# Moving the carry of the last 64 tokens' keys and values from ScalarE to SyncE's DMA queue

## The reference

```
xn = layernorm(x)
out = x + attn_block(xn) + ffn_block(xn)
```

```
q, k, v = split(shift_token(x) @ wqkv)          # 512 columns each
q, k = rotary_xpos(l2norm(q) * qs, l2norm(k) * ksc)
# windows of 64 tokens; each window's queries see the keys and
# values of their own window and of the window before
attn = softmax(mask(q k^T)); o = attn @ v
x = x + o @ wo
x = x + gated_ffn(layernorm(shift_token(x)))
```

## Time and profile before

| | |
|---|---|
| three runs, us | 990.7, 990.86, 988.4 (median 990.7) |
| the profiled execution, us | 988.95 |
| its span in the profile, us | 986.8 |
| busy: PE, DVE, ACT, POOL, us | 868.8, 685.1, 691.4, 623.8 |
| mean granted clock of TensorE | 0.98 |

### The profile page before, as it was taken

One profiled execution on the slowest core, in us unless ns is written; L12 is line 12 of the kernel. 1 busy time (PEld: TensorE's weight loads), 2 busy tenths in 40 slices (PEclk: granted clock), 3 DMA queues, 4 the chain that ended last, 5 costly groups with the idle time before them and its releaser, 6 DMA issues.

```text
span 986.8 us, 26415 instructions
## 1 busy us (share of the span) xinstructions
PE 868.8 (88%) x10836; PEld 582.5 (59%) x10836; DVE 685.1 (69%) x1129; ACT 691.4 (70%) x1419; POOL 623.8 (63%) x492
## 2 busy tenths in 40 slices
PE   1678889989899998998989889999999999999876
PEld 0346666666656666566666656565656565656552
DVE  5874665757667576675666877888787878797733
ACT  0456786877868777687786667777777777777643
POOL 4488676776767767767576566657575757575500
PEclk9979999999999999999999899999999999999987
DMA  9100000000000000000000000000000000000000
GB/s 291 28 1 3 2 2 2 2 3 2 3 2 1 3 1 3 2 2 3 1 3 2 1 1 2 2 12 12 13 12 7 17 2 22 1 23 2 22 23 11
DMA packets 20481, 13.47 MB, mean 14 GB/s; under 512 B 4578, under 2 KB 19596, under 8 KB 20236
## 3 DMA queue, kind: packets, MB, share of 16 engines
q1 hardware_dynamic: 15108, 10.49, 3.5%
q10 hardware_dynamic: 5256, 1.31, 0.8%
HBM read 9.70 MB, written 2.10 MB: 12 GB/s over the span
## 4 chain that ended last, share of the span: by engine, by line
PE 51%; DVE 23%; ACT 14%; issue 8%; POOL 3%; DMA 1%; DVEq 0%; POOLq 0%; SPq 0%; ACTq 0%
PE pQK L1172 6%; DVE m L711 6%; PE pS L1098 5%; PE pT L1083 4%; PE pT L1040 4%; PE pM L1115 4%; PE pV L1135 4%; PE pM L1245 4%; PE pS L1072 4%; PE pQK L1336 3%; DVE xa L899 2%; DVE ss L724 2%; DVE pr L759 2%; DVE mx L757 2%; PE pS L1059 2%
## 5 line engine op out<-in xcount | busy, mean ns | idle before, releaser
L355 POOL TENSOR_TENSOR rn<-rn,half_neg 128x16 f32<-128x16 f32 x64 | 187.5, 2929 | 5.3
L368 POOL TENSOR_TENSOR m<-m 128x1024 f32<-128x1024 f32 x64 | 151.0, 2359 | 1.0 <-DVE m L711 1.0
L353 POOL TENSOR_SCALAR rn<-ss 128x16 f32<-128x16 f32 x64 | 16.3, 255 | 205.1 <-DVE ss L724 203.9
L375 POOL TENSOR_TENSOR qkn<-m,rn 128x1024 f32<-128x1024 f32 x64 | 123.7, 1933 | 5.0
L757 DVE TENSOR_REDUCE mx<-pS 128x8 f32<-128x1024 f32 x64 | 78.1, 1220 | 66.7 <-PE pS L1072 66.6
L1172 PE MATMUL pQK<-wqkv,hT 128*128 128x512 f32 x256 | 123.5, 606 | 0.8 <-DVE m L711 0.8
L510 ACT ACTIVATE kT<-pT 128x512 f32<-128x512 f32 x64 | 38.1, 595 | 86.4 <-PE pT L1040 85.9
L550 ACT ACTIVATE sq<-pQK 128x1024 f32<-128x1024 f32 x64 | 65.4, 1021 | 25.7 <-PE pQK L1172 25.6
L724 DVE TENSOR_REDUCE ss<-sq 128x16 f32<-128x1024 f32 x64 | 77.5, 1210 | 5.4 <-ACT sq L550 5.3
L1098 PE MATMUL pS<-vmix,prT 128*64 128x65 f32 x1024 | 74.0, 226 | 7.4 <-DVE pr L759 7.4
L1098 PEld LDWEIGHTS pS<-vmix,prT 128*64 128x64 f32 x1024 | 65.3, 139 | 25.5 <-issue 20.8
(11 more groups left out here) (169 smaller groups left out, 2038.2 us busy)
## 6 DMA issues: line engine op xcount, KB each, us to landing
x<-in_L_attn_x SPq DMA_DIRECT2D x4, 512.0 KB, 9.4
xs<-in_L_attn_x SPq DMA_DIRECT2D x8, 256.0 KB, 2.8
out<-aqkT SPq DMA_DIRECT2D x8, 256.0 KB, 2.2
wqkv<-in_L_ffn_wqkv SPq DMA_DIRECT2D x2, 768.0 KB, 9.5
tab<-in_k_tab SPq DMA_DIRECT2D x1, 1024.0 KB, 10.5
w<-in_L_ffn_w SPq DMA_DIRECT2D x2, 341.0 KB, 10.3
wo<-in_L_ffn_wo SPq DMA_DIRECT2D x2, 256.0 KB
cst<-in_k_cst ACTq DMA_DIRECT2D x1, 404.5 KB, 4.0
```

The lines of the kernel that those rows point to most:

```text
L355: eng.tensor_tensor(rn[:, k % 2, :], rn[:, k % 2, :], half_neg[:, 0:2 * H], ALU.pow).then_inc(S["rn_done"], 1)
L368: eng.tensor_tensor(m1[:, k % 2, :], m1[:, k % 2, :], m2[:, :], ALU.add).then_inc(S["add_done"], 1)
L375: eng.tensor_tensor(qkn[:, k % 2, :].rearrange("p (h d) -> p h d", d=DH), m1[:, k % 2, :].rearrange("p (h d) -> p h d", d=DH), rn[:, k % 2 ...
```

## The change

The two copies leave ScalarE's stream. SP issues them as DMAs from SBUF to SBUF, one pair per tile from the second tile on, each behind a wait for the semaphore that ScalarE had waited for: o_mm for the values, s_mm for the keys. A completed DMA adds 16 to its semaphore, so ScalarE's two waits count in sixteens. The value DMA copies whole rows of 520 fp32 per partition (65 for each head, with the constant ones that form the softmax sum), where ScalarE copied 8 runs of 64. The key DMA copies 4 runs of 64 fp32 in each of 128 partitions. SP's loop over the output steps is written out over the bodies: `xs` is loaded at the start of the body, the body's four carries follow, and then the wait for `osb` and the store.

```diff
--- before.py
+++ after.py
@@ -298,6 +298,13 @@
             body(None, None, (1, NT - 1))
 
 
+        def sp_carry(sp, n, b):
+
+            sp.wait_ge(LS["o_mm"], n - 3)
+            sp.dma_start(vmix[b][64:P, :, :], vown[b][64:P, :, :]).then_inc(LS["v_kept"], 16)
+            sp.wait_ge(LS["s_mm"], n - 3)
+            sp.dma_start(kT[b][:, :, P:P + WIN], kT[b][:, :, WIN:P]).then_inc(LS["carried"], 16)
+
         @block.sync
         def _(sp):
             for b in range(NB):
@@ -312,16 +319,20 @@
                 sp.dma_start(w2[:, l, 0:2, :], a["L0_ffn_w2"][l, 0:2 * P, :].rearrange("(c p) d -> p c d", p=P)).then_inc(w_ld, 16)
                 sp.dma_start(w2[0:CHUNKS[2][1], l, 2, :], a["L0_ffn_w2"][l, 2 * P:HID, :]).then_inc(w_ld, 16)
 
-            sp.dma_start(xs[:, :, :], x_steps[0]).then_inc(G["xs"], 16)
-            sp.wait_ge(G["osb"], 1)
-            sp.dma_start(out_steps[0], osb[:, :, :]).then_inc(G["out"], 16)
-            with sp.Fori(1, NT) as t:
-                sp.wait_ge(G["out"], 16 * t)
-                sp.dma_start(xs[:, :, :], x_steps[t]).then_inc(G["xs"], 16)
-                sp.wait_ge(G["osb"], t + 1)
-                sp.dma_start(out_steps[t], osb[:, :, :]).then_inc(G["out"], 16)
+            def body(new, old, ff):
+                last = ff and ff[0] == 1
+                if last:
+                    need(sp, G["out"], 16 * ff[1])
+                    sp.dma_start(xs[:, :, :], x_steps[ff[1]]).then_inc(G["xs"], 16)
+                for k in range(NB):
+                    if new and not is_start(new):
+                        sp_carry(sp, count(new, k), k)
+                if last:
+                    sp.wait_ge(G["osb"], ff[1] + 1)
+                    sp.dma_start(out_steps[ff[1]], osb[:, :, :]).then_inc(G["out"], 16)
+
+            run_bodies(sp, body)
             sp.wait_ge(G["out"], 16 * NT)
-
 
         def pool_slot(eng, new, old, k):
 
@@ -506,22 +517,17 @@
                 step, b, m = turned
                 eng.wait_ge(S["t_mm"], 2 * m + 1)
                 if not is_start(step):
-                    eng.wait_ge(S["carried"], m - 3)
+                    eng.wait_ge(S["carried"], 16 * (m - 3))
                 eng.activation(kT[b][:, :, 0:P], pT[:, 512:1024].rearrange("p (c n) -> p c n", c=4), ACT.Copy).then_inc(S["t_ev"], 1)
                 eng.wait_ge(S["t_mm"], 2 * m + 2)
                 eng.activation(qT[:, :, :], pT[:, 0:512].rearrange("p (c n) -> p c n", c=4), ACT.Copy).then_inc(S["t_ev"], 1)
             if new:
-                if not is_start(new):
-
-                    need(eng, S["o_mm"], n - 3)
-                    eng.activation(vmix[k][64:P, :, 0:DH], vown[k][64:P, :, 0:DH], ACT.Copy).then_inc(S["v_kept"], 1)
-                    eng.activation(kT[k][:, :, P:P + WIN], kT[k][:, :, WIN:P], ACT.Copy).then_inc(S["carried"], 1)
                 if k < NB - 1:
                     act_shift(eng, new, k + 1)
 
                 eng.wait_ge(S["v_mm"], n + 1)
                 if not is_start(new):
-                    eng.wait_ge(S["v_kept"], n - 3)
+                    eng.wait_ge(S["v_kept"], 16 * (n - 3))
                 values = pV[:, :].rearrange("p (h d) -> p h d", h=H)
                 eng.activation(vown[k][:, :, 0:DH], values, ACT.Copy).then_inc(S["v_ev"], 1)
                 eng.activation(vmix[k][0:64, :, 0:DH], values[0:64], ACT.Copy).then_inc(S["v_ev"], 1)
```

## The result

| | before | after |
|---|---|---|
| median (lowest to highest), us | 990.19 (988.4 to 990.86), 4 runs | 983.28 (982.85 to 984.26), 4 runs |
| the profiled execution, us | 988.95 | 983.27 |
| its span, us | 986.8 | 981.1 |
| busy ACT, us | 691.4 | 635.5 |

The ratio is 0.9934, with a 95% interval of 0.9917 to 0.9952: the change saves 4.8 to 8.2 us, by the medians 6.9, by the two spans 5.7. The forecast was 986.4 us, 4.3 under the median that it started from, 990.7. As a ratio to the kernel before it lies just inside the second, whose low end is 983.5 / 990.7 = 0.9927; the median of before has come down to 990.19 with a fourth run.

What follows compares the result with a forecast made beforehand. TensorE was taken as busiest, with ScalarE's copies on the chain in six slots only: 6 x 0.69 = 4.1 us, other slots and DMA waits 0. From 988.95, 984.85; against median 990.7, 986.6; forecast 986.4, own range 984.5 to 988.

Steps and rivals of the forecast that it cites:

- the second: Whole kernel: the range to hold 8 in 10, 983.5 to 991 us.
- What bounds the kernel, and where ScalarE is on the chain: TensorE is busiest; the chain passes through ScalarE's copies only in slot 1 of layer 1's last six bodies.
- ScalarE's saving, 1.0 us per slot: ScalarE's queue: removing both copies shortens it by 1.0 us per slot, some 60 us over 60 slots.
- The 0.69 us per slot: Layer 1's six slots: the output projection L1115 loses its 0.69 us idle wait for oT, 4.1 us in all.
- The remaining 0.3 us disappears behind L1172: Layer 1's six slots: of ScalarE's 1.0 us, 0.3 us isn't paid out, since L1115 must follow projection L1172.
- more than 0.69 us is paid out: Rival, chance 0.07: ScalarE's whole 1.0 us gained in six slots, 6.0 us, 984.7 us; needs L1172 to end earlier.
- 54 slots at nothing: The other 54 of 60 carries gain 0 us; ScalarE's gain runs into waits on PE in the same slot.
- The DMA at 2.3 us, bounds 1.9 to 3.0: The value carry's SBUF-to-SBUF DMA on SP: taken as 2.3 us, bounds 1.9 to 3.0, at cost 0.
- every allowance: Time from o_mm until a late vown costs: about 3.8 and 4.1 us in layer 0, 3.9 and 4.4 in layer 1.
- The late-carry rival: Rival, chance 0.09: late value DMAs hold up ScalarE; sign turns at about 4.1 us, 999 us at 4.5.
- Given back or hidden: Rival, chance 0.22: a DVE or POOL collision behind L1115 eats the 0.69 us; time 988 to 991 us.

Runs made afterwards that it cites:

- two trips: Changed kernel with each value carry made twice by SP, the second copy behind the first one's landing: 1014.32 us, ratio 1.0256 to the kernel before.

## Why the prediction was right in kind and too small

- *What bounds the kernel, and where ScalarE is on the chain* (six slots): right. 6 of the 60 pairs give the full gain, the other 54 give a ratio of 1.0001.
- *ScalarE's saving, 1.0 us per slot*: 1.10 us measured in the six, since hT overlaps qT. This didn't change the sum, which PE's queue limits.
- *The 0.69 us per slot, "6 x 0.69 = 4.1 us"*: this is the term that was put too small. It is 0.96, and 6 x 0.96 = 5.8 us. The prediction ended L1172 at 744.37 + 1.88 = 746.25 and let L1115 start there; the next group really starts 1.72 us after L1172's start, at 746.09, and takes 1.05 instead of 1.16 us. "The remaining 0.3 us disappears behind L1172" was therefore 0.14 of 1.10: one copy alone pays out all of it, up to the 0.96.
- *The rival "more than 0.69 us is paid out"* (6.0 us, 984.7) came nearer in its size, but its condition, an earlier end of L1172, isn't what happened. L1172 is as long as before, and the room was behind its shown end.
- *54 slots at nothing*, with the waits at prT growing by 1.0 (by 1.06 in layer 0's slot 3): right, though the prediction had read only three kinds of slots; that the others give nothing is what the run with 54 pairs moved shows, to within 1 us.
- *The DMA at 2.3 us, bounds 1.9 to 3.0*: the carries landed after 2.2 and 2.3 us at the median and 3.1 and 3.3 at the longest, a little over the upper bound; every allowance held. The estimate of 2.3 us for the value carry by the Trainium skill ("DMA: Bandwidth & Descriptors", section "Anatomy of one DMA") is within 0.1 us of the 2.2 measured; that section is about DMAs that GpSimd issues, and these are issued by SyncE, so the agreement may be luck. By the rule on runs under 512 bytes in the same page of the Trainium skill (section "Specifications") the key carry with its 256-byte runs was to be the slower of the two: it is, by 0.1 us. The two differ in the number of runs and of partitions as well, so no run here shows that the rule is the reason.
- *The late-carry rival* did not come. Its threshold near 4 us is consistent with two trips at 4.5 us being slower, but 999 us at 4.5 us was too low: that kernel takes 1014 us.
- *"Given back or hidden"* did not come: all of the 0.96 arrives at `mx` of the next slot, and at the end.

The sum with the measured term is 988.95 - 5.8 = 983.15 for the profiled execution, which took 983.27; that they meet so closely is in part luck, as said above of the spans. By medians the gain is 6.9 us; the 1.1 us between is inside the interval, and no cause is given to it.

## What to carry to other kernels

Work taken off an engine is worth what it takes off the chain and no more than the next engine's queue allows: here 10% of 56 us. What a stall costs is read by comparing starts with the same pair of instructions where nothing is held up; the idle time in the bracket was 0.27 us less than the stall cost. Before offloading to a DMA, look for something that need not stand ahead of the critical instruction in the same slot: moving one table load gave the whole gain here. And slack left on an engine can be spent: a reorder that gave nothing before gave some 2.9 us with the carries gone (983.28 to 980.35, in two sets of runs whose medians of the kernel before are 0.2 us apart; the size is rough).

## What the runs showed of the hardware that was not expected

- Small copies from SBUF to SBUF on SP's queue land after 2.2 us (130 KB in 64 runs of 2080 bytes) and 2.3 us (128 KB in 512 runs of 256 bytes). Issuing takes 0.46 and 0.63 us; one key carry, issued right behind its value carry, took 1.60. The short runs cost 0.1 us in landing and 0.17 in issuing.
- A landing can be late. With two trips, seven second trips took 3.2 to 4.1 us instead of 2.2. In each of these windows the DMA view shows a transfer on the instruction queue; this one, of the kernel with two trips, has the carry at 319.43 us:

```profile
q8 instruction: 1, 0.02, 1.1%
...
vmix<-vown SPq DMA_DIRECT2D x1, 130.0 KB, 3.9
```

  In the changed kernel the latest value carry, 3.1 us at 381.92, has one as well. But in at least six windows with such a transfer the value carry landed after 2.2 to 2.4 us. The two go together; that one causes the other wasn't tested.
- Four matmuls of 128x512 fp32 let the next group start 1.72 us after their start though they are shown with 1.88, and eight matmuls whose operand comes late take 1.16 us instead of 1.05.
- TensorE's granted clock was 0.77 from 61 to 76 us in the changed kernel and 0.95 before, in the start-up where no carry had moved yet; the changed kernel lost some 2 us there in its profile and still ended 5.7 us earlier. In the nine other kernels the clock of this stretch is 0.77 to 0.89, and the two of them that leave all carries on ScalarE have 0.89, less than before as well.
